# Two small products behind each edge job, and one PSUM bank for the upper products, in a two-layer graph network kernel

## The reference, cut to what matters

```
agg = jnp.zeros_like(x).at[row].add(edge_attr)          # layer 0: 100000 x 256 into 6250 x 256, by src
h = relu(concat([x, agg, x_with_cond]) @ W1.T + b1) @ W2.T + b2
...
ht = relu(h @ W1 + b1)                                   # layer 1
msg = sigmoid(exp(w_param) * ht[src] + b_param)
fsum = segment_sum(msg, dst, num_segments=num_nodes)     # 100000 x 256 into 6250 x 256, by dst
s = clip(fsum, 1e-06, 0.9999999)
c = (log(s / (1.0 - s)) - b_param) / exp(w_param)
bundle = concat([ht, c]) @ Wn + bn                       # ht @ Wn[:256] + bn is the "upper product"
out = h_in + relu(bundle / norm(bundle))
```

## Time and profile before

| | |
|---|---|
| median of 3 runs | 2870.13 us (2869.02 to 2873.31) |
| the profiled execution's own time | 2868.22 us |
| its span | 2866.5 us |
| mean granted TensorE clock | 0.864 of full speed |
| PE / DVE / POOL / ACT busy | 72% / 67% / 61% / 45% of the span |

### The profile page before, as it was taken

The page is one execution under the profiler, slowest core; times in us unless marked ns, Lnnn a source line. Parts: engine busy times, 40 slices in busy tenths (PEclk is TensorE's granted clock), DMA queues, the critical chain, the costliest instruction groups (busy, mean ns, idle before and its releaser), DMA issues.

```text
span 2866.5 us, 34135 instructions
## 1 busy us (share of the span) xinstructions
PE 2071.8 (72%) x8433; PEld 1340.2 (47%) x8433; DVE 1914.2 (67%) x5018; ACT 1304.0 (45%) x4298; POOL 1746.8 (61%) x1674
## 2 busy tenths in 40 slices
PE   1489856667767776867997576877787786786784
PEld 0356633434434443534786353544543453454453
DVE  1578844765776875777786487577677677653378
ACT  0245423435534633634436243553563463374465
POOL 1568877767676666665015666667666666666503
PEclk9789967878888987989998688888898898898798
DMA  9989868435533333332447333333333333334434
GB/s 381 252 179 209 170 104 242 113 91 137 129 93 88 92 91 89 90 92 73 154 149 261 93 96 91 102 98 92 103 99 91 104 97 90 97 119 122 121 117 162
DMA packets 182549, 370.71 MB, mean 129 GB/s; under 512 B 33244, under 2 KB 101622, under 8 KB 179781
## 3 DMA queue, kind: packets, MB, share of 16 engines
q0 software_dynamic: 93168, 219.39, 30.6%
q1 hardware_dynamic: 77991, 114.14, 12.4%
q10 hardware_dynamic: 11200, 35.00, 3.2%
HBM read 281.76 MB, written 99.74 MB: 133 GB/s over the span
## 4 chain that ended last, share of the span: by engine, by line
PE 39%; DVE 22%; issue 18%; another core or an unknown queue 10%; ACT 3%; SPq 3%; DMA 2%; POOL 1%; DVEq 1%; ACTq 0%; POOLq 0%
PE bank L1474 37%; DVE agg L1229 9%; DVE hits L1156 2%; DVE oh L1160 1%; SPq L476 1%; DVE store L1160 1%; DVEq L1221 1%; ACT oh L832 1%; DVE store L1410 1%; DVE hit L1152 1%; DVE cum L1113 1%; POOL agg_copy L666 1%; ACT dist L824 1%; POOL store L692 1%
## 5 line engine op out<-in xcount | busy, mean ns | idle before, releaser
L1474 PE MATMUL bank<-store,oh 128*128 (+2 forms) x4610 | 1352.3, 427 | 463.1 <-DVE agg L1229 167.9
L1474 PEld LDWEIGHTS bank<-store,oh 128*128 128x128 f32 (+1 forms) x4610 | 809.0, 196 | 899.8 <-issue 450.9
L1229 DVE TENSOR_TENSOR agg<-bank,agg 128x256 f32 x1845 | 773.9, 419 | 506.8 <-PE bank L1474 253.0
L692 POOL DMA_INDIRECT store<-g_table,idx_all x785 | 769.2, 980 | 387.1 <-issue 179.5
L832 ACT ACTIVATE oh<-dist 128x128 f32<-128x128 f32 x1845 | 498.3, 301 | 1051.7 <-PE bank L1474 620.0
L692 POOL DMA_INDIRECT store<-in_edge_attr,idx_all x628 | 623.1, 992 | 284.9 <-issue 146.2
L824 ACT ACTIVATE dist<-iota,nloc_all 128x128 f32<-128x128 f32 x1845 | 582.8, 386 | 73.1 <-DVE nloc_all L1201 42.2
L666 POOL DMA_INDIRECT agg_copy<-agg x160 | 263.7, 1648 | 152.2 <-ACT agg L789 57.7
L1474 PE MATMUL bank<-oh,hit 125*128 125x314 f16 x720 | 154.6, 343 | 47.7 <-DVE oh L1160 36.8
L1156 DVE TENSOR_TENSOR hits<-iota,ttab 125x628 f16<-125x628 f16 x360 | 171.4, 476 | 0.0
L1160 DVE TENSOR_TENSOR oh<-hits,v 125x628 f16<-125x628 f16 x360 | 166.2, 479 | 3.2
(11 more groups left out here) (206 smaller groups left out, 1852.2 us busy)
## 6 DMA issues: line engine op xcount, KB each, us to landing
agg_copy<-store ACTq DMA_DIRECT2D x4, 6400.0 KB
agg<-in_edge_attr SPq DMA_DIRECT2D x39, 512.0 KB
agg_copy<-agg_copy POOLq DMA_DIRECT2D x16, 800.0 KB
store<-g_table,idx_all POOLq DMA_INDIRECT x785
store<-in_x SPq DMA_DIRECT2D x48, 256.0 KB
store<-in_edge_attr,idx_all POOLq DMA_INDIRECT x628
pre_scratch<-store SPq DMA_DIRECT2D x25, 256.0 KB
agg<-agg_copy SPq DMA_DIRECT2D x25, 256.0 KB
```

Source lines behind the costliest of these rows:

```text
L692: gp.indirect_dma_start(out=store[:, at % RING * D:(at % RING + 1) * D], out_offset=None, in_=table_dram, in_offset=bass.IndirectOffsetOnA ...
L1229: dve.tensor_tensor(to, pt[n % TB][:, 0:D], to, ALU.add).wait_op(s_mm, n + 1, "sem-ge").then_inc(s_acc, 1)
L1474: return pe.matmul(o, l, r, start=start, stop=stop, skip_group_check=skip)
```

## The change

Behind each of the 1845 jobs, TensorE issues two products (`FILLERS = 2`) of 32 columns of a zero matrix (`zr`, f16, 128 partitions) with themselves. They write a 32x32 corner of bank 7 (`pB`), and nothing reads it. They wait for nothing and nothing waits for them. Since `pB` is now written by them, the upper products all go to `pA` (bank 6); so the first half of chunk n has to wait for ACT's copy of chunk n-1, where it had to wait for the copy of chunk n-2. ACT's copy stands one or two quads sooner in ACT's order, and the store of a chunk 7 steps behind its second half in SP's order, where it stood 18 steps behind.

```diff
+FILLERS, FILL = 2, 32
...
-            at = HT_STEPS[2 * n + 1][0] * TILES + HT_STEPS[2 * n + 1][1] + 18
+            at = HT_STEPS[2 * n + 1][0] * TILES + HT_STEPS[2 * n + 1][1] + 7
...
-                HT_QUAD[min((NTH[jobs_at(1, g, t)[-1]] + OHS + 2) // QUAD + 1, -(-len(ORDER) // QUAD) - 1)] = n
+                HT_QUAD[min((NTH[jobs_at(1, g, t)[-1]] + OHS) // QUAD, -(-len(ORDER) // QUAD) - 1)] = n
...
-                act.copy(w2T[:, :], (pA, pB)[n % 2][:, :]).then_inc(s_qo, 1)
+                act.copy(w2T[:, :], pA[:, :]).then_inc(s_qo, 1)
...
-                if n >= 2:
-                    pe.wait_ge(s_qo, n - 1)
-                to = (pA, pB)[n % 2][:, j * D:(j + 1) * D]
+                if n:
+                    pe.wait_ge(s_qo, n)
+                to = pA[:, j * D:(j + 1) * D]
...
                 mm(pt[n % TB][:, 0:D], ohv[:, n % OHS, :], store[:, bass.ds(slot, D)], True, True
                    ).wait_op(s_oh, n + 1, "sem-ge").then_inc(s_mm, 1)
+                for _ in range(FILLERS):
+                    mm(pB[0:FILL, 0:FILL], zr[:, 0:FILL], zr[:, 0:FILL], True, True)
```

## The result

The changed kernel takes 3023.89 us (median of 4 runs, 3016.89 to 3036.14) where the kernel before took 2871.72 us beside it: ratio 1.0528, 95% interval 1.0508 to 1.0549, so 152 us or 5.3% slower. The forecast was 2903 us with a range to 2955. The side was right and the size was not; the rival "much slower", 3000 us, came nearest.

The account below looks back on a forecast made before the run. The prediction saw a loop of handovers with PE holding about 37% of the chain. Fillers +40, clock -7, bank and stores 0 gave +33 us on 2868.2, so 2901, forecast 2903 us as median, range 2846 to 2955.

Parts of the forecast that it names:

- much slower: Rival: handovers pass the delay from job to job, PE's 139 us charge counts in full, about 3000 us; chance 0.10.
- The bound: Two tile stages, 2095 us: a loop of handovers where PE holds about 37%; added PE time counts where no pause absorbs it.
- The cost of a job in contact: Jobs whose weights follow earlier work without pause pay 0.14 us more at high clock, 0.25 at low, for streaming and bare load.
- The upper bound that the prediction gave: Each job in contact pays 0.20 us (high clock) or 0.35 (low) if fillers took 0.06 us twice and the load came bare.
- The signs: Right: job idle below 423 us, PE share up, clock 0.86 to 0.88; wrong: clock 0.92 or more, or copy waits over 10 us.
- The sign that names the mechanism: In PE's runs of jobs in contact: passes still 0.215 us apart within a job, but 0.35 us from one job to the next.
- The number of jobs in contact: Tile stages: 1845 jobs less 987 weight-load pauses, each taken as one waiting job, leaves 858 without a pause.
- The fifth at the low clock: Of the 858 jobs in contact, a fifth, 172, was put at the low clock, because low stretches are thin.
- The cover by DVE: High-clock jobs in bursts: a third of the charge taken off, as DVE's 0.545 us add is late anyway; 24 us left.
- The clock: Tile stages: 6% more columns cut the 630 us of low clock by 38 us, giving -7 us on the path.
- the rival of a faster kernel: Tile stages: three quarters of low-clock time goes, net -24 us, 2846 us; faster from some 300 us gone; chance 0.27.
- One bank and the earlier stores: Upper products' single bank and earlier copies and stores: taken as 0 us, from a range of -12 to +14.

Follow-up runs that it names:

- e3: Changed kernel with both fillers given all 128 columns of zero weights, still 32 columns streamed; 2630.15 us, ratio 1.0021 to the kernel before.
- e1: Changed kernel without the two fillers, one bank and earlier copies and stores kept; 2626.75 against 2624.92 us for the kernel before, ratio 1.0014.
- e8: Kernel before with the sort's column counts using 128 columns of weights instead of 49; 2625.35 us, ratio 0.9992 to the kernel before.
- e4: Changed kernel with one filler per job, 128 columns of zero weights and 256 columns streamed; 2628.71 us, ratio 1.0012 to the kernel before.
- e6: Changed kernel with three fillers per job, each 128 columns of zero weights and 256 columns streamed; 2714.45 us, ratio 1.0337 to the kernel before.
- e2: Changed kernel with one 32-column filler behind each job instead of two; 2746.45 us, ratio 1.0470 to the kernel before.
- e9: Changed kernel with both fillers given 96 columns of zero weights instead of 32; 2942.83 against 2898.11 us for the kernel before, ratio 1.0150.

## Why the prediction was wrong, point by point

**The bound.** That PE holds the largest share of a chain of handovers, and that added time counts where no pause takes it up, held: its share went up, to 63.5%.

**The cost of a job in contact** is the step that failed: the prediction charged no wait for the change of width. The prediction charged 0.03 us for the fillers and 0.11 for the bare weight load, 0.14 us, and 0.25 at the low clock. The bare load was right in size (0.105 us, and 0.16 at the low clock where I had 0.22), and so was the streaming (0.038). What was missing is the wait at the change of width, 0.094 us in front and about as much behind: measured 0.34 and 0.47 us. e3, which has no such change, shows 0.14 us. The upper bound that the prediction gave, 0.20 and 0.35, did not hold the value either; its own words, 0.06 twice and the bare load of 0.11, make 0.23. The wait was to be read in the trace of before, around the 49-column counts, but the prediction never set two starts beside each other at a change of shape.

**The signs.** The share of the chain, the clock (0.87), the idle time before the job's products (423 to 259 us) and their mean (445 to 463 ns) came as said, and none of the signs of being wrong did. The sign that names the mechanism failed: 0.215 us within a job and 0.35 between jobs were announced, and 0.320 and 0.45 were measured. Even without a change of width (e3) it is 0.299 and 0.27: the load that comes bare is that of the job's second pass.

**The number of jobs in contact** was too small as well. Of the 987 pauses of the weight loads only 695 stand before a job's load, by the single records; the others stand before products of the sort and the upper products, though each was taken as a job. That leaves some 1150 jobs, not 858. By itself this would have moved the forecast by 13 us (+46 in place of +33). The fifth at the low clock was near: 305 of all 1845 jobs before, 17%.

**The cover by DVE.** The prediction took a third off, because a job at 0.57 us is hardly slower than an add at 0.545. With 0.14 us that is what e3 shows, 0.2%. With 0.34 us the pitch is 0.77 and the cover is gone. Worse, the jobs in bursts that DVE paced at 0.555 us, which I had counted as free, now run at 0.77 too: the weight load's idle 0.26 us held only some 0.13 us of real slack. With the right charges my own sum would have been 686 x 0.34 + 172 x 0.47 = 314 us of PE's time, 37% of it 116, minus 7: +109 us. The remaining 43 us to the 152 could be those formerly free jobs. But with 1150 jobs the same sum is 920 x 0.34 + 230 x 0.47 = 421 us, close to the 416 us that PE is busy more, and 37% of it less 7 is +149 without them. Both are worked out, with a share of 37% that no run tests, and the split stays open.

**The clock.** The -7 us rested on 6% more columns. In the first measurement the clock of the stages rose by 0.01, and by the mean clocks of the two spans the time at the low level fell from some 780 to 770 us, not by the 38 us of the prediction. In the sets of e1 to e8 it rose by much more (e4, e6), but never by so much that it paid for the products that brought it. In e6 some 320 us of the low time were gone, more than the 300 at which the prediction let the kernel become faster, and it was 88 us slower. With this falls the rival of a faster kernel. What the higher clock is worth alone is not shown; the smaller loss of e6 against e2 suggests that it counts once the pitch is over the add's pace. The Trainium skill, "TensorE: Matmul & The Clock Gate", section "Why this matters for your kernels", asks to keep TensorE free of idle gaps for the clock. e4 agrees that the clock follows (0.94 and 0.95), and its time stayed the same (1.0012).

**One bank and the earlier stores.** Charged 0 of -12 to +14; e1 shows +0.14%, some 4 us. Right.

**Much slower.** Its 3000 us came near the 3024 by luck. It let a charge of 139 us count in full; by the measured pitches the charge is 314 to 421 us, and 152 of it reached the end.

## What to carry to other kernels

Before putting a small product between large ones, look up in the trace what the array does at a change of shape: the start-to-start time across the change, on both sides, not the product's duration. A product for filling should keep the rows and columns of its neighbours; with 128 columns it cost 0.14 us a job here, with 32 columns 0.34. And count a charge against the pace of the next engine: pitches of 0.515 and 0.54 us a job were free beside an add of 0.55, 0.57 nearly, 0.59 cost 1.5% in its set, and 0.75 to 0.77 cost 3.4% or more. A higher granted clock is no gain by itself: none of the products that raised it here paid for themselves. Ask first whether the engine at the upper clock would still be the late one.

## What the runs showed that I had not expected

The wait at a change of shape: 0.094 us at the high clock and 0.137 at the low (0.564 against 0.427) between a 128x128 product and one with 32 or 49 columns, or 32 or 9 rows of weights (0.309 to 0.312 against 0.215), none with 96 columns. Between two products of the same narrow shape there is no such wait: fillers follow each other in 0.038 us (0.028 with 128 columns), and counts in 0.069 with 49 columns as with 128. The records of the weight loads say the same: behind a job's pass, the load of 32 or 49 columns, or of 32 rows, begins only with its own product (0.31 us behind the pass's start), and the load of 96 or 128 columns begins with the pass in front (e9, e3, e8). What in TensorE makes it so is not shown.

The kernel before has two levels of time in different sets of runs, with medians of 2870 to 2898 us and of 2625 to 2627 us. The waits of ACT in the trace of before, and then of e1 (which does the same work and ran at the lower level):

```profile
ACT oh L832 <- PE bank L1474: 620.0, 468, 19.7
ACT oh L832 <- remote: 272.9, 93, 15.8
```

```profile
ACT oh L833 <- PE bank L1475: 745.8, 640, 18.2
ACT agg L790 <- PE bank L1475: 82.5, 58, 17.4
```

At the upper level ACT stood 93 times, 273 us in total, for something that the profile does not show, and at the lower level such waits do not appear. In their place e1 has waits of PE for the gathers' transfers, 213 us where before has 17; whether these are the same waits under another name, and what makes the levels, stays open. Each ratio is within one set, but a loss of one set need not carry over to the other: the changed kernel itself lost 5.3% at the slower level and 5.0% at the faster.
